# Grouped attention: the key side folded from 32 rows of 512 columns to four groups of 32 rows of 128

## What is computed

```python
h = rmsnorm(x, ln1_w)
q = (h @ Wq).reshape(b, s, 16, 8)
k = (h @ Wk).reshape(b, s, 4, 8)      # 4 key heads of width 8: 32 rows in all
v = (h @ Wv).reshape(b, s, 4, 8)
q, k = apply_rope(q, cos, sin), apply_rope(k, cos, sin)
k, v = repeat(k, 4), repeat(v, 4)
scores = q @ k.T / sqrt(8), causal
out = softmax(scores) @ v @ Wo
```

## Time and profile before

| | |
|---|---|
| three runs, median (lowest, highest) | 3173.91 us (3171.54, 3180.02) |
| the profiled execution | 3171.85 us, of which the span is 3170.1 us |
| PE matmul busy | 2899.1 us, 91% |
| PE weight load busy | 1873.3 us, 59% |
| DVE busy | 2456.5 us, 77% |
| ACT busy | 2318.3 us, 73% |
| POOL busy | 2089.5 us, 66% |
| mean granted TensorE clock | 0.957 |

### The profile page before, as it was taken

The page is one execution under the profiler, slowest core; times in us unless marked ns, Lnnn a source line. Parts: engine busy times, 40 slices in busy tenths (PEclk is TensorE's granted clock), DMA queues, the critical chain, the costliest instruction groups (busy, mean ns, idle before and its releaser), DMA issues. The chain is left out here.

```text
span 3170.1 us, 66211 instructions
## 1 busy us (share of the span) xinstructions
PE 2899.1 (91%) x22258; PEld 1873.3 (59%) x22258; DVE 2456.5 (77%) x6944; ACT 2318.3 (73%) x3601; POOL 2089.5 (66%) x2402
## 2 busy tenths in 40 slices
PE   6999996899888988789589999999999999999979
PEld 3555553444444444678346666666666666666658
DVE  5666666888877874567468888888888888888867
ACT  5888872566556657444279999999999999999933
POOL 5666664346546543677657878877887788778744
PEclk8999997899989999899789999999999999999989
DMA  4454444221221230585400000000000000000001
GB/s 121 131 131 113 107 124 85 57 65 45 69 68 48 66 69 19 177 273 166 131 1 1 17 1 17 1 7 11 1 17 1 17 1 17 1 16 1 1 14 41
DMA packets 151510, 178.31 MB, mean 56 GB/s; under 512 B 18620, under 2 KB 122785, under 8 KB 151077
## 3 DMA queue, kind: packets, MB, share of 16 engines
q1 hardware_dynamic: 142084, 157.14, 18.9%
q0 software_dynamic: 9088, 16.94, 1.5%
HBM read 99.82 MB, written 75.95 MB: 55 GB/s over the span
## 5 line engine op out<-in xcount | busy, mean ns | idle before, releaser
L3364 PE MATMUL lb_FF<-lb_h,lb_w 128*128 128x512 f32 x1024 | 501.2, 592 | 0.0
L3593 DVE TENSOR_SCALAR lb_z<-lb_M,lb_mv,lb_rstd 128x128 f32<-128x128 f32 x1024 | 344.9, 399 | 3.3 <-POOL lb_rstd L3518 3.0
L3481 ACT ACTIVATE lb_h<-lb_H,lb_prm 128x512 f32<-128x512 f32 x512 | 326.6, 697 | 2.6 <-PE lb_H L3355 2.6
L3518 POOL TENSOR_TENSOR lb_rstd<-lb_rstd,half 128x4 f32<-128x4 f32 x256 | 260.4, 1017 | 37.2 <-issue 1.3
L3349 PE MATMUL lb_H<-lb_x1s,lb_w 128*128 128x512 f32 x512 | 272.1, 531 | 0.8 <-issue 0.8
L3364 PEld LDWEIGHTS lb_FF<-lb_h,lb_w 128*128 128x128 f32 x1024 | 193.5, 189 | 89.5 <-issue 61.1
L544 ACT ACTIVATE ga_PT<-ga_S 128x384 f32<-128x384 f32 x256 | 111.6, 488 | 179.2 <-PE ga_S L355 179.1
L3585 DVE BATCH_NORM_STATS2 lb_stats<-lb_M 128x6 f32<-128x128 f32 x1024 | 227.1, 284 | 13.0 <-PE lb_M L3308 7.9
L1640 POOL TENSOR_SCALAR_AFFINE_SELECT da_PT<-da_PT 128x1024 f32<-128x1024 f32 x128 | 143.7, 1123 | 114.3 <-ACT da_PT L1558 113.6
L3350 PE MATMUL lb_H<-lb_x1s,lb_w 128*128 128x512 f32 x512 | 202.9, 396 | 0.0
L3355 PE MATMUL lb_H<-lb_x1s,lb_w 128*128 128x512 f32 x512 | 202.8, 397 | 0.1
(11 more groups left out here) (514 smaller groups left out, 8846.1 us busy)
## 6 DMA issues: line engine op xcount, KB each, us to landing
moe_w<-experts_dram SPq DMA_DIRECT2D x39, 384.0 KB, 3.3
da_qT<-da_stq SPq DMA_DIRECT2D x64, 192.0 KB, 4.1
da_kT<-da_stk SPq DMA_DIRECT2D x64, 192.0 KB, 4.5
moe_x<-moe_xs SPq DMA_DIRECT2D x39, 260.0 KB, 3.5
tc_g<-moe_ys SPq DMA_DIRECT2D x32, 256.0 KB, 4.7
ga_q<-ga_stq SPq DMA_DIRECT2D x20, 384.0 KB, 5.6
lb_split<-moe_parts SPq DMA_DIRECT2D x8, 896.0 KB, 6.2
da_stq<-da_parts SPq DMA_DIRECT2D x16, 384.0 KB, 2.4
```

The costliest lines, as they stand in the source:

```text
L3364: pe.matmul(FF[:, :], w2[:, k, :], h[:, k, :], start=(k == 0), stop=(k == KC - 1)).then_inc(ff_filled, 1)
L3481: act.activation(h[:, k, :], H[:, k % 2, :], ACT.Gelu_apprx_tanh, bias=col(FB1 + k, i)).then_inc(h_ready, 1)
L3518: pool.tensor_tensor(out[:, :], out[:, :], C["half"][:, 0:NT], ALU.pow).then_inc(done, 1)
L3593: last = v.tensor_scalar(z[:, t, :], M[:, t * P:(t + 1) * P], mv[:, t, 0:1], rstd[:, t:t + 1], ALU.subtract, ALU.mult)
```

## The change

The key side is folded onto all 128 partitions. project_kk makes two products of 256 columns, for tokens 0 to 255 on partitions 0 to 63 and for the others on partitions 64 to 127. rotate_k multiplies 128 x 256. sum_k makes four products of 128 columns, one for each quarter of the tokens, onto partitions 0 to 31, 32 to 63, 64 to 95 and 96 to 127. The copy, the casts, the subtractions are 128 x 128 instead of 32 x 512. Each of the three stores becomes four, one for each quarter; their pieces are of 256 bytes. The table and the constant are loaded again in folded form by two new DMAs at the head of SP's program, with a semaphore of their own, fold_loaded, that rotate_k and sum_k wait for.

```diff
+    K_STORES = 16 * 3 * NT
...
+        k_rope = sb("k_rope", [P, SEQ // 2])
+        pair_sum = sb("pair_sum", [P, KV * HD])
...
-        rotK = sb("rotK", [2 * KV * HD, SEQ])
-        restK = sb("restK", [KV * HD, SEQ])
+        rotK = sb("rotK", [P, SEQ // 2])
+        restK = sb("restK", [P, P])
...
-        partsK = sb("partsK", [KV * HD, 3, SEQ], BF16)
+        partsK = sb("partsK", [P, 3, P], BF16)
...
-                pe.matmul(M[0:2 * KV * HD, :], wk[:, :], xnT[:, :], start=True, stop=True
-                          ).then_inc(kk_filled, 1)
+                for half in range(2):
+                    last = pe.matmul(M[64 * half:64 * half + 64, 0:SEQ // 2], wk[:, :],
+                                     xnT[:, SEQ // 2 * half:SEQ // 2 * (half + 1)],
+                                     start=True, stop=True)
+                last.then_inc(kk_filled, 1)
...
-                pe.matmul(M[0:KV * HD, :], pair_sum[:, :], rotK[:, :], start=True, stop=True
-                          ).then_inc(k_summed, 1)
+                pe.wait_ge(fold_loaded, 32)
+                for t in range(NT):
+                    r = slice(64 * (t // 2), 64 * (t // 2) + 64)
+                    last = pe.matmul(M[32 * t:32 * t + 32, 0:P], pair_sum[r, :],
+                                     rotK[r, t % 2 * P:(t % 2 + 1) * P], start=True, stop=True)
+                last.then_inc(k_summed, 1)
...
-                act.activation(restK[:, :], M[0:KV * HD, :], ACT.Copy).then_inc(sum_copied, 1)
+                act.activation(restK[:, :], M[:, 0:P], ACT.Copy).then_inc(sum_copied, 1)
...
-                v.tensor_tensor(rotK[:, :], M[0:2 * KV * HD, :], k_rope[:, :], ALU.mult
+                v.wait_ge(fold_loaded, 32)
+                v.tensor_tensor(rotK[:, :], M[:, 0:SEQ // 2], k_rope[:, :], ALU.mult
...
-                    v.wait_ge(k_stored, 48 * (c - 1))
+                    v.wait_ge(k_stored, K_STORES * (c - 1))
...
-                sp.dma_start(stk[c % 2, :, 0:3, :], partsK[:, 0:3, :]).then_inc(k_stored, 16)
-                sp.dma_start(stk[c % 2, :, 3:5, :], partsK[:, 0:2, :]).then_inc(k_stored, 16)
-                sp.dma_start(stk[c % 2, :, 5:6, :], partsK[:, 0:1, :]).then_inc(k_stored, 16)
+                for t in range(NT):
+                    r, cols = slice(32 * t, 32 * t + 32), slice(t * P, (t + 1) * P)
+                    sp.dma_start(stk[c % 2, :, 0:3, cols], partsK[r, 0:3, :]).then_inc(k_stored, 16)
+                    sp.dma_start(stk[c % 2, :, 3:5, cols], partsK[r, 0:2, :]).then_inc(k_stored, 16)
+                    sp.dma_start(stk[c % 2, :, 5:6, cols], partsK[r, 0:1, :]).then_inc(k_stored, 16)
...
-                sp.wait_ge(k_stored, 48 * c)
+                sp.wait_ge(k_stored, K_STORES * c)
...
+            sp.dma_start(k_rope[:, :], C["k_rope_halves_dram"]).then_inc(fold_loaded, 16)
+            sp.dma_start(pair_sum[:, :], C["pair_sum_halves_dram"]).then_inc(fold_loaded, 16)
```

More of the change, by code:

```diff
@@ L72, in grouped_attention @@
         wout = sb("wout", [P, P])
-        wq, wk, wv, rope, k_rope, pair_sum = (
-            G[n] for n in ("wq", "wk", "wv", "rope", "k_rope", "pair_sum"))
+        wq, wk, wv, rope = (G[n] for n in ("wq", "wk", "wv", "rope"))
+        k_rope = sb("k_rope", [P, SEQ // 2])
+        pair_sum = sb("pair_sum", [P, KV * HD])
         stats = sb("stats", [P, NT, 6])
@@ L120, in grouped_attention @@
         ones_loaded = sem("ones_loaded")
+        fold_loaded = sem("fold_loaded")
         scales_ready = sem("scales_ready")
@@ L3841 @@
     }
+    arrays["k_rope_halves"] = np.concatenate([arrays["k_rope"][:, :T // 2], arrays["k_rope"][:, T // 2:]], 0)
+    arrays["pair_sum_halves"] = np.tile(arrays["pair_sum"], (2, 1))
     nc = bacc.Bacc("TRN2", target_bir_lowering=False, num_devices=1)
```

## The result

The changed kernel takes **3195.27 us** (median of five runs, 3187.75 to 3202.52) against 3173.91 (five runs as well, 3171.54 to 3180.02): a ratio of 1.006, 95% interval 1.0048 to 1.0072. It is slower, by 21 us, and 3 us outside the range that was forecast. The profiled execution took 3195.27 us; its span is 3193.5 us, 23.4 more than before.

What follows compares the result with a forecast made beforehand. PE was the nearest bound, in a loop through DVE's query split and POOL's rotation. Gains of 7.2 us against losses of 4.2, 2.6 and 1.5 gave about +1 us: 3175 us, range 3155 to 3192.

Steps and rivals of the forecast that it cites:

- Part 1: DVE's key split in grouped attention: 512 elements per lane become 128, saving 0.8 us per block, all on the path.
- Parts 2 and 3: rotate_k, ACT's copy and POOL's third_k shrink; PE's sum_k and project_kk may shorten; all outside the loop, worth 0.
- Part 4: SP's nine more DMA issues per block ahead of both loads: everything lands 3.0 us later, partly covered by spare time.
- more long SP issues: Long SP issues falling in the exposed stretch, about one block in four: three more blocks at 0.5 us, +1.5 us.
- rival A: Slower: loads 4.6 us or more late, PE stops at mask s = 4 in every block; 3191 to 3196 us; chance 0.19.
- 0.5 left: Spare us before PE's mask at s = 4 in a covered block: 4.3 - 0.8 - 3.0.
- the prediction's own rule: A block whose loads have under 3.0 us to spare before PE's mask loses 3.0 minus that spare.
- rival B: Slower: longer first PE wait and a third at s = 4 lengthen the half-speed stretch; +12 us, 3187; chance 0.12.
- Rival C: Faster: with PE's second wait at 0.9 us the clock stays up in most blocks; 3169, or 3152 to 3153; chance 0.24.

Runs made afterwards that it cites:

- fold3: Changed kernel with its folded compute, but keys stored by three DMAs from all 128 partitions and read back by eight loads instead of two: 3169.89 us, ratio 0.9978.
- b12cols: Kernel before with each of its three key stores cut into four by columns, twelve stores of 256-byte pieces, old compute: 3205.14 us, ratio 1.0094.

## Why the prediction was wrong

**Right.** Part 1: L782 took 0.29 us (0.29 forecast), L784 0.23 (0.21), L780 0.75 (0.7 to 0.8), and it ends at 846.99, 0.08 us after POOL's third_q:

```profile
845.75 1.16 POOL L651 TENSOR_TENSOR ga_partsQ<-ga_rotB,ga_partsQ 128x512 bf16<-128x512 f32 x1 [1.80 <-DVE ga_partsQ L795]
```

The cast of a quarter of the columns takes 0.75 us where the second cast of the same size takes 0.23, and ends when POOL's instruction has ended: with the rule on the shared port pair in the Trainium skill ("SBUF — State Buffer") the trace agrees. PE's second wait fell by the 0.8 us forecast (1.68 to 0.86). Parts 2 and 3 were rightly costed at nothing: POOL's rotation still ends the wait of the query split (2.37 us), and nobody waits for rotate_k or the sum. In Part 4 the single issue (0.43 + 0.04 us), the start of the key stores 4.5 us after the cast and the burst's length without a long issue (10.1 - 4.5 = 5.6 us, forecast 5.4) were right.

**Wrong, first: the size of Part 4's term "more long SP issues".** I had seen one (L1005, 1.88 us) and priced all that would come at about one block in four, as part of 1.5 us in the whole stage. It came in 12 of 15 blocks. A long issue costs 0.8 to 1.5 us, so that instead of 3.0 the loads came 3.5 us later on average (the key loads went out 12.1 us after the query cast, 11.3 forecast). That is just where the prediction itself had put the threshold of rival A, "it decides from about 3.5 us of delay on". The 3.0 us was itself too near the edge: blocks 2, 3 and 4 have no long issue, and PE waits there too (0.15, 0.94 and 0.27 us). In block 4 the keys land 3.1 us later than before, much as forecast, but PE is at the mask 1.1 us sooner and not 0.8, so that the "0.5 left" is gone. And the sum left a block out: it priced the first and the 13 from the third on, while the second had 1.6 us to spare; by the prediction's own rule it loses 3.0 - 1.6 = 1.4 us, and it lost 1.67.

The trace of before held what would have sized the long issues. Its DMA view counts 47 "instruction" packets in blocks 2 to 13, 558.6 us, one in 11.9 us, and SP issues for some 4.7 us of a block (six stores and four loads): 4.7 / 11.9 of 15 blocks is 6, and 4 were hit (with the one of 0.99 us). With nine stores more it issues for 8.9 us: 8.9 / 11.9 of 15 is 11, and 12 were hit.

**Wrong, second: no place was left for rival B inside rival A.** I had priced the late loads and the falling clock apart, 0.19 and 0.12. They come together: blocks 3, 10, 11 and 12 pay about 1.4 us each for a low stretch behind the new wait, some 5 us. Per block PE spends 7.7 us at the lower level and not 6.5. With the waits themselves (7.3 us in blocks 3 to 13) this eats more than the 0.8 us per block that the split gives. Of the two signs that B named, the third wait came and the longer first one didn't (1.69 us in place of 1.62). The first block lost 3.55 us where 2.6 was forecast, again one long issue.

**Wrong, third: the sum ended with the stage.** It had no term for the stages behind it, and 11.1 of the 23.4 us arose there, over half of that in the ternary stage. No row of before bears a price for this. But the diff had an added wait per block on DVE, which the prediction doesn't price; it takes nothing in the stage where it stands, and moves the instructions behind it along DVE's stream. Without the 11.1 us from behind the stage the median would have been about 3184: inside the range, and still slower. So the number missed the range by the ternary stage, and the mechanism was wrong in any case: 12.7 us of loss in the stage where about 1 was forecast, and PE waiting for the loads in most blocks, which the prediction had named as the sign that it is wrong.

Rival A's mechanism is what happened, in a milder form: SP's time, by long issues and not by 0.6 us for each store, and not the time of the pieces. Its 3191 to 3196 holds the measured 3195; that agreement is in good part luck, since A knew nothing of the 11.1 us behind the stage. Rival C's clock recovery did exist, but only where the stores were kept to three: fold3's stage is 17.3 us shorter.

**Open.** Whose instructions the packets beside the long issues carry, and whether they cause them or only share a cause; whether the 2.2 us more in the collecting stage and in the linear blocks are more than spread; what makes DVE pause at a fixed record of its stream; why only some of PE's waits at s = 4 are followed by the lower clock; which of the executions behind the medians have the long ternary stage.

## What to carry to other kernels

When a layout is folded over more partitions, count the DMAs that take it apart again, and see if the buffer on the other side can be reordered so that one DMA still takes all partitions: here three stores of 128 rows cost SP 1.4 us and twelve of 32 rows 5.6, and with that a gain of 17 us in the stage became a loss of 13. Where a queue's spare time is within 1 us of a forecast delay, price the case in which it is used up together with what the engine's clock does behind the new wait. And compare the stages that were not changed too: a wait that is fulfilled for good takes no time where it stands, but it moves all later instructions along the engine's stream, and its price, or its gain, may stand in another stage.

## What was not expected of the hardware

- One SP issue in most blocks takes 1.2 to 1.9 us in place of 0.42, and each of the 13 in the changed kernel stands beside a 16 KB packet of the queue "instruction".
- SP's time for the issue of a store grows little with the rows: 0.295 us for 8 rows, 0.32 to 0.43 for 32, 0.38 to 0.62 in the median for 128, each without the long issues; whether a row is one piece of 1024 bytes or pieces of 256 made no difference (0.42 to 0.43 either way; for the first key store of a block 0.32 us with rows of 3072 bytes and 0.33 with pieces of 256, b12cols).
- In the changed kernel waits of PE of 0.9 to 1.3 us at s = 4 were followed by 3.4 us at the lower clock (0.50) in four blocks; waits of 0.15 to 0.6 us were not, and one of 1.22 us (block 8) and one of 1.57 (block 1) weren't either.
- Fifteen fulfilled waits on DVE in one stage moved the length of another, 1,770 us later, between 121 and 130 us, without a change in any instruction there: a pause of 0.20 us stood before the same record of DVE's stream in six kernels, and it shifted DVE against POOL for the rest of the stage, 7.97 us a step in place of 7.24.
